# Moving sixteen row tiles of the third image from the last image's attention into the wait for its sorted rows, with a buffer of their own for those rows

## The chip, the core and the metric

The kernel runs on one core of a Trainium2 chip. The metric is the device time of one execution in microseconds. TensorE (PE), VectorE (DVE), ScalarE (ACT), GpSimd (POOL) and SyncE (SP) each run their own list of instructions in order and meet at semaphores. SyncE issues the plain DMAs, GpSimd the indirect ones.

## The reference

Four images of 32 x 32 positions with 128 channels pass three residual blocks, all in float32:

```
x = x + conv(gn(x))            # deformable 3x3 sampling, 8 groups, projected back
t = t + attn(ln(t))            # slices: softmax over the tokens, 8 heads of 32
t = t + moe(ln(ln(t)))         # 8 experts 128 -> 512 -> 128, the best 2 of each token

logits = xt @ Wr + br; top_p, top_idx = top_k(softmax(logits), 2)
xe = xn * ln_g[e] + ln_b[e]
h  = gelu(xe @ W1[e] + b1[e]);  y = h @ W2[e] + b2[e]
out = sum over the two experts of weight * y
```

## The kernel before

The images go through the kernel one after another, and the stages of neighbouring images are woven. Each engine runs one list in which the deformable sampling (conv) of image b is cut into 80 slots, and into these slots the attention, router and expert work of image b - 1 and the last parts of image b - 2 are put. After the last image's conv there is no more conv to weave into: there a tail of slots runs in which `tail_works(slot)` gives two pieces of work, image 3 at table slot `slot + 3` and then image 2 at `slot + 80`.

The tables at the top of the file say at which slot a step stands, and each engine's `work(b, slot)` issues what the tables name. For image 3 the order is: layer norm, the transposes of its normalised tokens, attention (slots 5 to 28), a second norm, the router (35 to 40), ranks and row numbers (43), columns and the b2 product (44 to 47), the scatter of the rows (44 to 55), the load of the rows (56), their transposes and scalings (61 to 63), row tiles (64 to 87), picks (89 to 100), adds (101 to 105).

The expert part works on rows sorted by expert. 1024 tokens with two experts each fill at most ROWS = 23 tiles of 128 rows, each tile of one expert. Its steps, all named in the prediction:

- find_rows (L1738) gives each token its two row numbers (L1760) and each tile its expert.
- sort_rows (L692, POOL, L702) scatters the normalised tokens to `sorted_rows` in DRAM, 16 indirect DMAs of 64 KB.
- load_weights(b, i) (L559, SP, L571 and L573) loads the two weight matrices of tile i's expert, 256 KB each, to a ring. Images 0 to 2 have a ring of 4; image 3 has 12, since 8 more lie in the conv's `asb`, which is free by then. Image 3's first 12 are all issued at WEIGHT_SLOT 45, each further one when a tile before it is done.
- load_rows (L577, SP, L582) brings the sorted rows to SBUF in three pieces. It waits for the scatter and for image 2's results having been stored, since rows come in and results go out through one buffer, `rows_in = rows_out` in `region`.
- turn_rows (L1076, PE, L1083) transposes 4 tiles at a time; scale_rows (L1790, DVE, L1795) applies the expert's norm scale and shift.
- tile(b, i) (L1115, PE) is hidden(i), the four products of L1098, and finish(i - 1), the four of L1111. Between them stands gelu(b, i) (ACT, L1325). After them copy_rows (DVE, L1801). For images 0 to 2 the hidden product has one PSUM bank, so hidden(i) waits for the Gelu of tile i - 1. For image 3 it has four.
- store_rows_out (L588, SP, L590) stores the results in three pieces, pick_rows (L706, POOL, L712) gathers them back in token order, 16 indirect DMAs, and add_rows (L1803, DVE, L1811) adds them with their weights. store_image (L555) ends an image.

The tiles of image 2 (LATE) stand in the tail, at slots 2 to 40 of it, that is 5 to 43 in image 3's table: within image 3's attention and router. Attention steps named in the prediction are the token transposes (L956), logits (L1002, L1003), the two Exps (L1316), the slice sums (L1020), the add of the attention (L1654), the router's transposes (L1040), the ranks (L1053, L1056) and the b2 product (L1072). Between image 3's b2 product and its turn_rows TensorE has nothing in its list.

## Time and profile before

| | |
|---|---|
| median of 3 runs | 1411.14 us (1404.44 to 1413.74) |
| the profiled execution | 1399.52 us |
| its span, first to last instruction | 1397.3 us |
| mean granted TensorE clock | 0.876 |
| busy PE, DVE, ACT, POOL | 75%, 58%, 56%, 48% of the span |
| DMA | 111.11 MB, 80 GB/s on average |

All rows are from the profiled execution, in microseconds from the start of its span. The execution's own time is 2.2 us more than its span and lies below the three timed ones. "Granted clock" is a share of TensorE's full clock: 1.00 is 2.4 GHz and 0.50 is 1.2 GHz.

### The profile page before, as it was taken

What the parts mean: (1) busy time and instruction counts of PE and PEld (TensorE: products, weight loads), DVE (VectorE), ACT (ScalarE), POOL (GpSimd) and SP (SyncE); (2) the same over time, 40 slices, a digit from 0 to 9 for tenths busy, and PEclk for the clock granted to TensorE, in tenths of its full rate; (3) what the DMA queues carried; (4) which work ended last, traced back from release to release, by engine and by line L of the source; (5) the groups of instructions that cost most, each with busy time, mean ns of one, the idle gap of its engine ahead of it and who ended that gap; (6) DMA issues with size and microseconds to landing.
All of it is one profiled execution on the core that took longest, in us unless ns stands there. A gap on an engine that the chain in (4) does not pass through costs nothing.

```text
span 1397.3 us, 51058 instructions
## 1 busy us (share of the span) xinstructions
PE 1050.7 (75%) x22444; PEld 840.0 (60%) x22444; DVE 812.6 (58%) x1609; ACT 786.5 (56%) x1435; POOL 675.3 (48%) x640
## 2 busy tenths in 40 slices
PE   4586858877877878998788679988878776983390
PEld 3465646655565657874577558865656565673390
DVE  5767676756658456565668455566775484434221
ACT  2766666665667355766665636665674553552060
POOL 2755555555445664436645744367456650004404
PEclk9697978988999789999987889999996989997595
DMA  6302121211001332641112125531112201446462
GB/s 159 97 22 53 63 52 63 53 65 36 23 15 31 88 90 83 182 115 41 39 35 86 38 71 151 164 90 30 38 35 85 82 17 32 137 126 197 127 211 58
DMA packets 150524, 111.11 MB, mean 80 GB/s; under 512 B 44009, under 2 KB 131874, under 8 KB 149794
## 3 DMA queue, kind: packets, MB, share of 16 engines
q1 hardware_dynamic: 146210, 99.47, 25.7%
q0 software_dynamic: 4096, 8.40, 2.1%
q8 instruction: 178, 2.92, 0.8%
q14 instruction: 40, 0.33, 0.1%
HBM read 84.17 MB, written 23.66 MB: 77 GB/s over the span
## 4 chain that ended last, share of the span: by engine, by line
PE 54%; ACT 16%; DVE 14%; issue 8%; POOL 3%; SPq 2%; DMA 2%; another core or an unknown queue 1%; POOLq 0%; DVEq 0%; ACTq 0%
PE ps L866 14%; PE ps L850 10%; PE ps L1098 6%; PE ps L874 5%; ACT xsb L1240 5%; PE ps L1111 5%; DVE asb L1572 4%; ACT asb L1258 2%; DVE region L1795 2%; DVE xsb L1549 2%; PE ps L1020 2%; PE ps L823 2%; DMA ring<-in_L_ffn_W 1%; DVE ysb L1563 1%; ACT xsb L1234 1%
## 5 line engine op out<-in xcount | busy, mean ns | idle before, releaser
L741 POOL TENSOR_TENSOR ysb<-ysb,rw 128x576 f32<-128x576 f32 x300 | 336.5, 1143 | 362.4 <-DVE ysb L1563 362.3
L850 PE MATMUL ps<-xsb,ysb 64*64 64x96 f32 x11008 | 340.4, 270 | 100.3 <-issue 25.1
L850 PEld LDWEIGHTS ps<-xsb,ysb 64*64 64x64 f32 x11008 | 283.6, 149 | 170.2 <-issue 97.4
L1240 ACT ACTIVATE xsb<-xsb,pick 128x576 f32<-128x576 f32 (+1 forms) x480 | 336.2, 750 | 5.2
L1572 DVE COPY asb<-ps 128x960 f32<-128x960 f32 (+1 forms) x208 | 215.7, 1043 | 131.0 <-PE ps L866 120.0
L730 POOL TENSOR_TENSOR ysb<-rw,count 128x576 f32<-128x576 f32 (+1 forms) x150 | 176.0, 1173 | 99.2 <-PE ps L850 98.6
L866 PE MATMUL ps<-asb,vd 32*32 32x258 f32 x8192 | 203.0, 393 | 17.3 <-issue 13.8
L1249 ACT ACTIVATE osp<-ps 128x258 f32<-128x258 f32 x128 | 43.0, 444 | 268.7 <-PE ps L866 268.7
L1325 ACT ACTIVATE region<-ps,b_col 128x128 f32<-128x128 f32 x368 | 105.0, 370 | 137.4 <-PE ps L1098 137.3
L866 PEld LDWEIGHTS ps<-asb,vd 32*32 32x32 f32 x8192 | 126.4, 104 | 82.5 <-issue 51.0
L1549 DVE TENSOR_TENSOR xsb<-rw,ps 128x576 f32<-128x576 f32 (+1 forms) x150 | 108.3, 722 | 75.2 <-PE ps L850 57.7
L702 POOL DMA_INDIRECT sorted_rows<-region,row_no x64 | 63.1, 985 | 133.0 <-DVE row_no L1760 116.4
L1234 ACT ACTIVATE xsb<-xsb 128x576 f32<-128x576 f32 (+1 forms) x160 | 105.3, 658 | 21.2 <-DVE xsb L1549 21.2
L1563 DVE SCALAR_TENSOR_TENSOR ysb<-ysb,ps 128x576 f32<-128x576 f32 (+1 forms) x158 | 113.6, 719 | 3.0 <-POOL ysb L730 3.0
L1098 PE MATMUL ps<-region,ring 128*128 128x128 f32 x616 | 93.9, 300 | 27.3 <-ACT region L1325 15.4
L1258 ACT ACTIVATE asb<-ps 128x768 f32<-128x768 f32 x112 | 93.8, 837 | 33.9 <-PE ps L850 28.7
L1098 PEld LDWEIGHTS ps<-region,ring 128*128 128x128 f32 x616 | 81.5, 206 | 39.8 <-issue 29.3
L712 POOL DMA_INDIRECT picked<-expert_rows,row_no x64 | 61.1, 954 | 72.7 <-DMA expert_rows<-region 55.4
L874 PE MATMUL ps<-outw,osp 128*128 128x128 f32 x512 | 78.6, 317 | 12.8 <-issue 7.8
L1581 DVE TENSOR_TENSOR x_tok<-x_tok,ps 128x1024 f32<-128x1024 f32 x32 | 39.0, 1218 | 83.2 <-PE ps L874 80.0
L1111 PE MATMUL ps<-ring,region 128*128 128x128 f32 x616 | 84.2, 281 | 4.0 <-ACT region L1325 4.0
L874 PEld LDWEIGHTS ps<-outw,osp 128*128 128x128 f32 x512 | 72.4, 226 | 18.5 <-issue 14.7
(260 smaller groups left out, 1169.5 us busy)
## 6 DMA issues: line engine op xcount, KB each, us to landing
ring<-in_L_ffn_W SPq DMA_DIRECT2D x154, 256.0 KB
vd<-group_values SPq DMA_DIRECT2D x128, 128.0 KB, 2.7
asb<-in_L_ffn_W SPq DMA_DIRECT2D x30, 256.0 KB
set_rows<-ring SPq DMA_DIRECT2D x4, 1376.0 KB, 6.6
rw<-set_rows SPq DMA_DIRECT2D x30, 172.0 KB, 3.5
group_values<-region SPq DMA_DIRECT2D x32, 128.0 KB, 3.5
region<-sorted_rows SPq DMA_DIRECT2D x8, 512.0 KB
expert_rows<-region SPq DMA_DIRECT2D x8, 512.0 KB
```

Of the source, the lines that this page charges most:

```text
L730: pl.tensor_tensor(ysb[:, ch % DEPTH, 0:sets, NU - 1, :], rows_of(ig)[:, 1, first:first + sets].rearrange("p (s o) -> p s o", o=1) .broadc ...
L741: pl.tensor_tensor(ysb[:, ch % DEPTH, 0:sets, u, :], ysb[:, ch % DEPTH, 0:sets, NU - 1, :], rows_of(ig)[:, 2 + u, first:first + sets].rear ...
L850: last = pe.matmul(ps[64 * j:64 * j + 64, bank + i, NV * GRID * q:NV * GRID * (q + 1)], ysb[rows, ch % DEPTH, col, :, :].rearrange("p u y ...
L866: last = pe.matmul(ps[32 * jc:32 * jc + 32, j, 0:NI * AM], vd[rows, ig % 2, x, :], asb[rows, x, :, :].rearrange("p i n -> p (i n)"), start ...
L874: last = pe.matmul(pcol(project_bank(ig), t), osp[:, ig % 2, t // 4, t // 2 % 2, t % 2 * P:(t % 2 + 1) * P], outw[:, ig % G, :], start=Tru ...
L1098: last = pe.matmul(ps[:, hidden_bank(b, i), j * P:(j + 1) * P], ring_part(r, 0)[:, j * P:(j + 1) * P], xsT[:, i, :], start=True, stop=True)
L1111: last = pe.matmul(ps[:, expert_bank(b, i), 0:C], hT[:, i % 2, j, :], ring_part(r, 1)[:, j * P:(j + 1) * P], start=(j == 0), stop=(j == HJ ...
L1240: act.activation(xsb[:, ch % DEPTH, 0:sets, v, :], xsb[:, ch % DEPTH, 0:sets, NV - 1, :], ACT.Relu, bias=pick[:, v:v + 1], scale=-1.0).the ...
L1258: act.activation(asb[:, :, :, first:first + m].rearrange("p x i m -> p i x m"), ps[:, bank:bank + 2, 0:GRID * m].rearrange("p i (m x) -> p ...
L1549: dve.tensor_tensor(xsb[:, ch % DEPTH, 0:sets, NV - 1, :], rows_of(ig)[:, 0, first:first + sets].rearrange("p (s o) -> p s o", o=1) .broad ...
L1563: dve.scalar_tensor_tensor(v, v, 0.0, units.rearrange("p (o q) -> p o q", o=1) .broadcast_to([P, sets, GRID]), ALU.max, ALU.min).then_inc( ...
L1572: dve.tensor_copy(asb[:, :, :, first:first + m].rearrange("p x i m -> p i x m"), ps[:, bank:bank + 2, 0:GRID * m].rearrange("p i (m x) -> ...
```

## The change

The tables: image 2's first eight tiles stay within image 3's attention and router, at other places (image 3's slots 5, 7, 17, 29, 30, 39, 40, 41), and the other sixteen entries stand at 45 to 60, after the b2 product and before turn_rows. Picks keep their slot number; the adds move by five slots and the store of image 2 by one. Image 3's first twelve weight loads are cut in three lots of four, at slots 52, 57 and 62. The ring numbering of image 3 is turned by four, so that its first eight tiles use the part in `asb`, which image 2 doesn't use, and don't wait for image 2's tiles. Image 3's rows get a place in the conv's `xsb` buffer, both on the way in and on the way out; load_rows then doesn't wait for image 2's stores. turn_rows of image 3 waits for image 2's last copy, as both use PSUM banks 6 and 7.

```diff
-LATE_TILE_SLOTS = tuple(SLOTS + 2 + 5 * i // 3 for i in range(ROWS + 1))
-LATE_PICK_SLOT, LATE_ADD_SLOT, LATE_LAST_SLOT = SLOTS + 53, SLOTS + 72, SLOTS + 82
+LATE_TILE_SLOTS = tuple(SLOTS - TAIL_FIRST + at for at in (5, 7, 17, 29, 30, 39, 40, 41) + tuple(range(45, 61)))
+LATE_PICK_SLOT, LATE_ADD_SLOT, LATE_LAST_SLOT = SLOTS + 53, SLOTS + 77, SLOTS + 83
+LAST_WEIGHT_SLOTS = {52: (0, 4), 57: (4, 8), 62: (8, 12)}
...
-        rows_in = region[:, REGION - ROWS * C:REGION].rearrange("p (i c) -> p i c", i=ROWS)
-        rows_out = rows_in
+        woven_rows = region[:, REGION - ROWS * C:REGION].rearrange("p (i c) -> p i c", i=ROWS)
+        last_rows = x_flat[:, 0:ROWS * C].rearrange("p (i c) -> p i c", i=ROWS)
+
+        def rows_of_tiles(b):
+            return woven_rows if b < B - 1 else last_rows
...
-            r = i % size
+            r = i % size if b < B - 1 else (i + RING) % size
...
             def load_weights(b, i):
...
-                elif b:
+                elif b and r < RING:
                     sp.wait_ge(s.expert_summed, ROWS * b)
...
             def load_rows(b):
                 sp.wait_ge(s.rows_sorted, 16 * TOP * NT * (b + 1))
-                if b:
+                if 0 < b < B - 1:
                     sp.wait_ge(s.expert_stored, 16 * 3 * b)
...
-                if slot == WEIGHT_SLOT:
+                if slot == WEIGHT_SLOT and b < B - 1:
                     for i in range(ahead):
                         load_weights(b, i)
+                elif slot in LAST_WEIGHT_SLOTS and b == B - 1:
+                    for i in range(*LAST_WEIGHT_SLOTS[slot]):
+                        load_weights(b, i)
...
             def turn_rows(b, q):
...
+                if b == B - 1:
+                    pe.wait_ge(s.expert_copied, ROWS * b)
```

`rows_of_tiles(b)` takes the place of rows_in and rows_out in load_rows, store_rows_out, turn_rows and copy_rows.

## Rows read from the trace of the kernel before

**Rows 1.** Stretches of the tail; us, engines busy (instructions), granted clock, DMA share, GB/s

```profile
1168.10:1272.00 103.90, 83.64 (x574) 71.34 (x574) 42.41 (x166) 54.57 (x125) 0.00 (x0) 0.93 0.38 107
1272.00:1310.90 38.90, 2.09 (x17) 1.90 (x17) 6.25 (x16) 0.81 (x1) 29.44 (x31) 0.56 0.82 242
1310.90:1321.00 10.10, 6.08 (x25) 4.59 (x26) 6.31 (x20) 0.00 (x0) 1.35 (x2) 0.50 0.37 94
1321.00:1364.40 43.40, 43.06 (x368) 42.71 (x367) 11.87 (x43) 26.23 (x92) 0.00 (x0) 0.96 0.57 170
1364.40:1397.30 32.90, 0.03 (x1) 0.00 (x0) 4.58 (x17) 0.00 (x0) 15.10 (x16) 0.57 0.22 62
```

**Rows 2.** Waits, 1168 to 1311 us: us in total, times, longest

```profile
PE ps L1083 <- DMA region<-sorted_rows: 35.9, 1, 35.9
...
PE ps L1098 <- ACT region L1325: 15.4, 10, 5.9
```

**Rows 3.** Timeline of GpSimd: start us, us; first and last of 16 scatters

```profile
1272.31 1.00 POOL L702 DMA_INDIRECT sorted_rows<-region,row_no  x1 [116.39 <-DVE row_no L1760]
...
1291.58 0.96 POOL L702 DMA_INDIRECT sorted_rows<-region,row_no  x1 [0.30 <-issue]
```

**Rows 4.** Timeline of SyncE's issues in the wait

```profile
1277.88 0.28 SPq L571 DMA_DIRECT2D ring<-in_L_ffn_W  x1
...
1279.42 0.35 SPq L571 DMA_DIRECT2D ring<-in_L_ffn_W  x1
...
1296.95 0.70 SPq L571 DMA_DIRECT2D asb<-in_L_ffn_W  x1
...
1303.25 0.70 SPq L571 DMA_DIRECT2D asb<-in_L_ffn_W  x1
...
1308.15 2.80 SPq L582 DMA_DIRECT2D region<-sorted_rows  x3
```

**Rows 5.** Groups of ScalarE's instructions, first stretch: busy us, mean ns, idle before

```profile
L1325 ACT ACTIVATE region<-ps,b_col 128x128 f32<-128x128 f32 x92 | 26.2, 368 | 29.6 <-PE ps L1098 29.5
L1325 ACT ACT_TABLE_LOAD x6 | 7.7, 1283 | 0.1
```

**Rows 6.** Timeline, marks of the attention chain

```profile
1182.62 1.04 PE L956 MATMUL ps<-ident,region 128*128 128x128 f32 x8
...
1202.58 1.02 PE L1002 MATMUL ps<-region,ws_bd 128*128 128x512 f32 x2
...
1216.59 1.15 ACT L1316 ACTIVATE xsb<-xsb,a_nmax 128x1024 f32<-128x1024 f32 x1
...
1229.89 4.92 PE L1020 MATMUL ps<-xsb 128*128 128x128 f32 x32
...
1241.64 1.22 DVE L1654 TENSOR_TENSOR x_tok<-x_tok,ps 128x1024 f32<-128x1024 f32 x1 [4.71 <-PE ps L1033]
...
1252.20 1.04 PE L1040 MATMUL ps<-ident,region 128*128 128x128 f32 x8
```

**Rows 7.** Timeline of VectorE, second reciprocal

```profile
1198.16 1.74 DVE L1618 RECIPROCAL ysb<-ysb 128x256 f32<-128x256 f32 x1
```

**Rows 8.** Stretches of 4 us between Exp and slice sums; columns as in rows 1

```profile
1222.00:1226.00 4.00, 1.54 (x13) 1.11 (x11) 1.27 (x7) 3.96 (x8) 0.00 (x0) 0.94 0.46 118
1226.00:1230.00 4.00, 3.65 (x17) 3.69 (x18) 0.00 (x0) 2.25 (x6) 0.00 (x0) 0.50 0.04 13
```

**Rows 9.** Timeline of TensorE, last woven tiles, ranks, b2 product

```profile
1263.52 1.13 PE L1098 MATMUL ps<-region,ring 128*128 128x128 f32 x8 [1.95 <-ACT region L1325]
...
1265.96 1.13 PE L1098 MATMUL ps<-region,ring 128*128 128x128 f32 x8 [0.43 <-ACT region L1325]
...
1267.83 0.34 PE L1053 MATMUL ps<-marks,earlier 128*128 128x72 f32 x2
...
1272.87 2.05 PE L1072 MATMUL ps<-b,region 8*128 8x128 f32 x16 [1.10 <-ACT region L1311]
```

**Rows 10.** Timeline of TensorE, first hidden products of the last image

```profile
1320.78 3.62 PE L1098 MATMUL ps<-region,ring 128*128 128x128 f32 x16
```

More of the change, by code:

```diff
@@ L578, in load_rows @@
                 sp.wait_ge(s.rows_sorted, 16 * TOP * NT * (b + 1))
-                if b:
+                if 0 < b < B - 1:
                     sp.wait_ge(s.expert_stored, 16 * 3 * b)
                 for q in range(3):
-                    sp.dma_start(rows_in[:, CHUNKS[q]:CHUNKS[q + 1], :],
+                    sp.dma_start(rows_of_tiles(b)[:, CHUNKS[q]:CHUNKS[q + 1], :],
                                  sorted_dram.rearrange("(i p) c -> p i c", p=P)[:, CHUNKS[q]:CHUNKS[q + 1], :])\
@@ L590, in store_rows_out @@
                 sp.dma_start(expert_dram.rearrange("(i p) c -> p i c", p=P)[:, CHUNKS[q]:CHUNKS[q + 1], :],
-                             rows_out[:, CHUNKS[q]:CHUNKS[q + 1], :]).then_inc(s.expert_stored, 16)
+                             rows_of_tiles(b)[:, CHUNKS[q]:CHUNKS[q + 1], :]).then_inc(s.expert_stored, 16)
             def work(b, slot):
                 ahead = RING if b < B - 1 else TAIL_RING
-                if slot == WEIGHT_SLOT:
+                if slot == WEIGHT_SLOT and b < B - 1:
                     for i in range(ahead):
+                        load_weights(b, i)
+                elif slot in LAST_WEIGHT_SLOTS and b == B - 1:
+                    for i in range(*LAST_WEIGHT_SLOTS[slot]):
                         load_weights(b, i)
@@ L1082, in turn_rows @@
                 for i in range(4 * q, min(4 * q + 4, ROWS)):
-                    last = pe.transpose(ps[:, 6 + q % 2, i % 4 * P:(i % 4 + 1) * P], rows_in[:, i, :], ident[:, :])
+                    last = pe.transpose(ps[:, 6 + q % 2, i % 4 * P:(i % 4 + 1) * P], rows_of_tiles(b)[:, i, :], ident[:, :])
                 last.then_inc(s.tiles_turned, 1)
@@ L1800, in copy_rows @@
                 dve.wait_ge(s.expert_summed, ROWS * b + i + 1)
-                dve.tensor_copy(rows_out[:, i, :], ps[:, expert_bank(b, i), 0:C]).then_inc(s.expert_copied, 1)
+                dve.tensor_copy(rows_of_tiles(b)[:, i, :], ps[:, expert_bank(b, i), 0:C]).then_inc(s.expert_copied, 1)
             def add_rows(b, m):
```

## The prediction

> **What bounds the kernel now.** I read the stretches first, then the waits, then the timeline around the last two images. In the tail there are five stretches [rows 1]. From 1168.1 to 1272 us the last image's attention and router run, woven with the third image's 23 row tiles; TensorE is busy 83.64 of 103.90 us. From 1272 to 1310.9 TensorE has 2.09 us of work in 38.90. Then come 10.1 us of turning the sorted rows, 43.4 us of the last image's tiles (TensorE busy 43.06) and 32.9 us of picks, adds and store. So the second stretch is a hole, and the first and the fourth are filled by TensorE. The waits name the hole: the first transposes of sorted rows wait 35.9 us for the DMA that loads them [rows 2]. Two things fill this time. GpSimd scatters 16 tiles' rows, from 1272.31, the last issued at 1291.58 [rows 3]. And SyncE has 24 weight loads ahead of the row load, which it reaches only at 1308.15, some 16 us after the last scatter [rows 4]. The rows could not go to their place earlier anyway without the third image's tiles being stored, since both use one buffer.
>
> A second reading of the first stretch matters more. A woven tile is not free there: ScalarE spends 26.2 us on 92 Gelu pieces and reloads its table for them six times at 1283 ns [rows 5], and TensorE's Gelu waits sum to 15.4 us [rows 2]. The attention is a chain, and every tile that stands in it beyond what the chain's own gaps can hold lengthens it.
>
> **The change part by part.** The sum goes by the profiled execution (1399.52 us, span 1397.3). Its time lies below all three timed runs (median 1411.14); I take the gain from its span and subtract it from the median.
>
> *Part A, 16 tiles leave the attention.* I lay the chain out again with the marks of [rows 6], one segment after another. Start to the transpose of the normalised tokens (1182.62): tile 2 goes, worth 2.1 us, as TensorE is slow here. To the first logits (1202.58, 19.96 us): five tiles stand there, one will. Four tiles at some 1.8 us (43.4 us for 23, [rows 1]) would be 7.1, but then the reciprocals' chain on VectorE (1.74 us each half, [rows 7]) ends last: 5.3. To the first Exp (1216.59, 14.0 us): two tiles between the logits and one Gelu go, the Exp table load follows the logits: 4.1. To the slice sums (1229.89, 13.3 us): here Exp and Gelu alternate. Two Gelus of 4 x 368 ns, the table loads between them and a tile go, and some 1 us comes as the transposes run slow (1.04 us at full clock, as at 1182.62): 5.2. (The parts that go add up to more than that; the chain Exp, transpose, copy, Exp, transpose, copy is what stays.) To the attention's add (1241.64, 11.75 us): a tile goes (1.8), sums run slower for longer: -0.3. To the transpose for the router (1252.20, 10.56 us): four tiles become two, 1.7. To the ranks (1267.83, [rows 9], 15.6 us): five tiles become three, but the transposes and router run at the slow clock: -1.2. From the ranks to the row numbers nothing changes. The sum is 16.9, and I take 17.
>
> The clock is the large unknown here. TensorE's granted clock was 0.94 in 1222 to 1226 with 1.54 of 4 us busy, and 0.50 in the next 4 us [rows 8]: a sparse stretch costs the following one half its speed (the 1.2 GHz level instead of 2.4). Before, 11 us at roughly half busy did it. After, between logits and sums TensorE has some 2 of 9 us of work, and again a gap of 4 us before the router's transpose. I have charged 6 us: half the sums (2.2), the transposes (2), the router (1.8; sixteen pieces, as in the b2 product's 2.05). If the clock stayed high the whole way, part A would be worth 22 to 23; if it stayed low from the logits to the ranks, every TensorE piece there doubles: sums and output product 3.8 each (32 pieces, four hidden products' worth of 0.95, [rows 9]), transposes 3, router 1.9, ranks 2 and 5 tiles at 1.1, in all 20 instead of 6, and part A is worth 3.
>
> *Part B, 16 tiles stand in the wait.* A lone tile in this form has a pitch of 2.44 us: hidden product at 1263.52, the next at 1265.96, since one PSUM bank makes it wait for its Gelu [rows 9]. The row numbers are ready at about 1272.0; the b2 product ends at 1274.92 and will end 2.3 us after the row numbers, as one tile's product no longer precedes it. Fifteen hidden products from there: the last starts 2.3 + 14 x 2.44 = 36.5 us after the row numbers. Its Gelu, second product and copy take 3.5: 40. The hole was 38.9 long, so on TensorE alone the hole is filled with nothing over, and the scatter (20.3 us) is no longer what ends last.
>
> *Part C, queues in that wait.* SyncE now holds, in order: late loads 11 to 17, four tiles of the last image (52), late loads 18 to 21, the three row loads (56), late load 22, four more tiles (57), the last store of the third image, and four more (62). One tile's two loads take about 1.6 us to issue (1277.88 to 1279.42, [rows 4]). Load 17 is released some 19 us after the row numbers; the four tiles behind it take 6.4, so load 18 is issued at 28 and lands at 31, while its product is due at 26.7: a stall of 4. Load 22 stands behind 1.5 MB of rows, another 2. The DMA itself can carry this: with 0.82 of it busy it moved 242 GB/s in the hole [rows 1], some 295 when full, and the tiles ask 0.52 MB per 2.44 us, 215 GB/s, plus 52 for the scatter (64 KB per 1.26 us). Part B becomes 46 us. Bounds: 40 with no stall, 52 if each late load waits a queue's length.
>
> *Part D, the buffer, the added wait and the turning.* The rows have their own buffer, so they land long before they are wanted. The transposes now wait for the copy of tile 22 instead; behind them on TensorE is everything of the last image. The turning took 9.9 us, until the first hidden products at 1320.78, at clock 0.50 [rows 1, 10]; 6.31 of it were VectorE's scalings, with a pause while the next rows and transposes came. With all rows there VectorE's scalings set it (some 0.32 us each, 6.31 for 20 pieces); TensorE's last transposes wait for sixteen of them, 5.2, and with the first and the last transposes it is 6.5. Hidden(0) thus starts 46 + 6.5 = 52.5 us after the row numbers, before 48.8. The fourth stretch starts warm: 1.9 less (3.62 us for the first two products, [rows 10], instead of twice 0.95).
>
> The clock gate rule of the Trainium skill (TensorE: Matmul & The Clock Gate, Part 4: PE-mode transpose) says that transposes do not count as activity for the clock. The trace agrees so far: all of the turning ran at 0.50 [rows 1]. By that rule the 1.9 of the warm start would be lost and the gain would be 13.
>
> *The rest.* The third image's picks (20 us on GpSimd) move into the last tiles; GpSimd has nothing else there, and they end about 67 us after the row numbers, before the adds at tile 16 (81). Their adds, 16 on VectorE, stand beside tiles that leave it idle most of the time (11.87 busy of 43.4, [rows 1]). The picks, adds and store at the end stay at 32.9. Moving them costs nothing unless the picks come 14 us late. The turned ring numbering only lets the last image's first eight tiles use the upper buffers.
>
> *Sum.* 17 (A) - 3.7 (B, C and the turning) + 1.9 (warm start) = 15.2, 15 us. Span 1382, that execution 1384.5; from the median 1411.1 - 15 = 1396.
>
> ScalarE's table price is another place where page and trace differ. Of ScalarE's 29.6 us of idle time ahead of Gelu pieces 29.5 are waits for TensorE [rows 5], so a load costs its 1283 ns and nothing more. The Trainium skill (ScalarE: Activation LUTs, What ACT_TABLE_LOAD costs) adds a drain of about 1380 ns to each switch; by it the five loads that go would bring up to 7 us more, an estimate from that page. I go by the trace.
>
> **The rivals.**
> *The clock eats it.* The attention without its tiles stays at the low level from logits to ranks. For it: [rows 8], and that it took only half-idle stretches before. Against: the sums and products are themselves 8 us of dense work, and the clock came back within 4 to 8 us of such work. Part A is worth 3 and the sum 1: 1410.
>
> *The SyncE queue becomes the bound, on the slow side.* From about 1295 to 1308 each SyncE instruction took some 0.70 us; the load at 1296.95 was followed by the next at 1303.25, a pitch of 6.3 us per tile, with the DMA far from full [rows 4]. It set in after some 12 closely spaced loads under GpSimd's indirect DMAs. Before, nobody waited for these loads but the row load. Now the third image's tiles do. If it sets in with the burst of slot 52, loads 18 to 22 have 6.3 instead of 2.44 (19 us), the row load adds 4 and its neighbour 4: 27 - 15, 12 slower: 1423. It decides against the change from the point where four loads are at that pace. Against it: loads are now released one per tile, and elsewhere with GpSimd busy SyncE was quick.
>
> *More than forecast.* The clock stays high, and the four-tile burst doesn't stall load 18: 22.5 + 2.3 - 1.9, and 4 more for the stall: 24 to 27 us, 1386.
>
> *It trades place for place.* If the hole had only been long because SyncE was slow (the rows could have been there at about 1298), a run in which it is quick gains 12 less: 1408.
>
> **How the numbers follow.** Forecast 0.52 (its own range 1389 to 1403), clock 0.14, trade 0.12, SyncE 0.08, more 0.14. Two in ten are cut off about equally on both sides: 1384 to 1411. A measurement here tells about 1% (14 us) from nothing. The forecast lies on that edge, so half of it counts as faster, with all of "more" and a little of "trade" (runs differ): 0.26 + 0.14 + 0.03, and I say 0.45. Slower is SyncE and the worst of the clock: 0.10. Same: 0.45.
>
> **What would show it.** Right: the row numbers come about 17 us earlier; the clock row shows a dip in the attention before the sums and before the router; Gelu's table loads fall from six to three; in the wait TensorE has some 2 us of 2.44 busy, with one pause near tile 18 and one near tile 22; the transposes of sorted rows wait for VectorE's copy or nothing, not for the DMA; the last 32.9 us unchanged. Wrong: row numbers less than 8 us earlier (clock), waits of TensorE for ring loads over 10 us in the wait (SyncE), or a hole that stays.

## The result, and the profile after

The changed kernel took 1436.99 us (median of 4 runs, 1429.37 to 1454.15), the kernel before beside it 1407.79 (1399.08 to 1413.74). The ratio, without slow executions such as the one of 1454.15 (in e4 and e5 it is the profiled one that was slow, but its extra time lies ahead of the tail), is 1.0163, 95% interval 1.0105 to 1.0222: slower, by one to two percent. 1396 was forecast, with 1384 to 1411 as the range. The profiled execution took 1434.3 us, its span is 1432.1; 1384.5 was forecast for it.

The five stretches of the tail, in the same cut as [rows 1]: the attention and router, the wait with its 16 tiles, the turning, the last image's tiles, and picks, adds and store. Columns: length, busy time of TensorE, its weight loads, VectorE, ScalarE and GpSimd with the number of instructions, granted clock, share of the DMA engines, GB/s.

```profile
1174.70:1262.40 87.70, 62.36 (x327) 49.28 (x328) 38.66 (x151) 32.18 (x60) 0.00 (x0) 0.79 0.15 43
1262.40:1333.10 70.70, 43.39 (x265) 40.74 (x265) 10.38 (x29) 17.10 (x60) 15.45 (x16) 0.78 0.69 200
1333.10:1339.80 6.70, 4.02 (x23) 3.03 (x24) 5.99 (x19) 0.00 (x0) 2.70 (x3) 0.83 0.90 242
1339.80:1399.10 59.30, 47.90 (x370) 47.13 (x368) 12.12 (x43) 26.12 (x92) 12.44 (x14) 0.85 0.55 159
1399.10:1432.10 33.00, 0.04 (x1) 0.00 (x0) 4.58 (x17) 0.00 (x0) 15.11 (x16) 0.55 0.22 62
```

Against before the attention is 16.5 us shorter (104.2 from its last convolution product to the row numbers, now 87.7), as forecast. The wait and the turning went from 48.4 to 77.4, where 52.5 was forecast. The last image's tiles went from 43.7 to 59.3, where 41.8 was forecast (43.7 less the 1.9 of the warm start). The end is the same. With 6.6 us more in the body ahead of the tail, which no edit touches and which differs by up to 31 us between the traces of this study (the tail starts between 1161.5 and 1192.2), these make the 34.8 us between the two spans. So the result stands in two places: the tiles in the wait, and the last image's tiles, from which nothing had been moved.

What the engines wait for there, as sums from 1174.7 us on (total, times, longest):

```profile
ACT region L1335 <- remote: 26.6, 3, 11.6
DVE xsb L1811 <- remote: 17.8, 2, 12.3
DVE region L1811 <- remote: 13.7, 1, 13.7
PE ps L1108 <- DMA ring<-in_L_ffn_W: 11.1, 2, 6.3
PE ps L1121 <- ACT region L1335: 9.4, 2, 9.1
```

"Remote" is a release that the profile can pin on no instruction of the core. ScalarE's Gelu (L1335) and VectorE's copy (L1811) wait so for 58 us in six waits; each counts from the engine's last instruction, so the first microseconds of it may be ordinary waiting for a product. The timeline of the wait shows where they stand (start us, us, engine, line):

```profile
1270.23 1.06 PE L1121 MATMUL ps<-ring,region 128*128 128x128 f32 x8
1270.93 0.71 SPq L576 DMA_DIRECT2D ring<-in_L_ffn_W  x1
1271.38 0.96 POOL L710 DMA_INDIRECT sorted_rows<-region,row_no  x1 [0.30 <-issue]
...
1275.97 1.14 ACT L1335 ACTIVATE region<-ps,b_col 128x128 f32<-128x128 f32 x4 [6.89 <-remote]
...
1277.25 2.05 PE L1108 MATMUL ps<-region,ring 128*128 128x128 f32 x8 [5.96 <-ACT region L1335]
...
1281.48 0.96 POOL L710 DMA_INDIRECT sorted_rows<-region,row_no  x1 [0.30 <-issue]
1285.17 0.29 DVE L1811 COPY region<-ps 128x128 f32<-128x128 f32 x1 [13.73 <-remote]
1285.19 1.14 ACT L1335 ACTIVATE region<-ps,b_col 128x128 f32<-128x128 f32 x4 [8.09 <-remote]
...
1285.61 2.05 PE L1121 MATMUL ps<-ring,region 128*128 128x128 f32 x8 [6.31 <-DVE region L1811]
```

The 16 scatters run from 1262.42 to 1282.44 without a gap but GpSimd's own 0.30 us. The tile before passes beside them at its usual pace. The product of the next tile ended at about 1270.4, yet its Gelu starts at 1275.97. A second product whose copy was due at about 1271.3 is copied at 1285.17, and at 1285.19 the next Gelu starts: both engines are let go together, 2.7 us after the last scatter. In these 14 us TensorE gets one hidden product done, and that one and the next at half clock (2.05 us for 8 pieces instead of 1.06).

The same again under the third image's 16 picks, which also run unbroken, 1336.49 to 1356.20:

```profile
1353.59 0.29 DVE L1811 COPY xsb<-ps 128x128 f32<-128x128 f32 x1 [12.27 <-remote]
...
1355.26 0.94 POOL L720 DMA_INDIRECT picked<-expert_rows,row_no  x1 [0.30 <-issue]
1359.28 2.17 ACT L1335 ACTIVATE region<-ps,b_col 128x128 f32<-128x128 f32 x8 [11.63 <-remote]
...
1360.47 2.07 PE L1121 MATMUL ps<-asb,region 128*128 128x128 f32 x8 [9.09 <-ACT region L1335]
```

Between the two stand TensorE's waits for weights, from the same timeline:

```profile
1305.26 0.37 SPq L578 DMA_DIRECT2D asb<-in_L_ffn_W  x1
1306.73 0.36 SPq L576 DMA_DIRECT2D ring<-in_L_ffn_W  x1
...
1311.25 2.08 PE L1108 MATMUL ps<-region,ring 128*128 128x128 f32 x8 [6.29 <-DMA ring<-in_L_ffn_W]
...
1316.66 3.66 SPq L587 DMA_DIRECT2D xsb<-sorted_rows  x3
1321.08 1.00 SPq L576 DMA_DIRECT2D ring<-in_L_ffn_W  x1
...
1327.36 2.08 PE L1108 MATMUL ps<-region,ring 128*128 128x128 f32 x8 [4.81 <-DMA ring<-in_L_ffn_W]
```

Each is a late load of the third image that SyncE issues only behind loads of the last image (the one at 1306.73 behind four tiles' loads, the one at 1321.08 behind the three row loads). These are the two pauses of part C, 4 and 2 us there.

In the kernel before the 16 scatters and the 16 picks of the third image made one train of 32, from 1272.3 to 1312.5, while TensorE, ScalarE and VectorE had next to nothing to do until 1310.9 [rows 1, 3]. What it held up was SyncE, whose slow instructions I had seen [rows 4] and read as a matter of SyncE, and at its end VectorE's last scalings (under part D).

### The profile page after: what moved, and what is told of

Same layout as the page of the kernel before. It is cut to its first block, busy times and chain, and to the rows that moved or that the text cites. A ratio compares the mean times of both kernels' runs of the same rounds, so it can differ in the third digit from the quotient of the medians.

```text
span 1432.1 us, 51055 instructions
## 1 busy us (share of the span) xinstructions
PE 1078.2 (75%) x22444; PEld 862.2 (60%) x22444; DVE 814.1 (57%) x1609; ACT 780.2 (54%) x1430; POOL 672.4 (47%) x640
## 4 chain that ended last, share of the span: by engine, by line
PE 55%; DVE 16%; ACT 15%; issue 7%; another core or an unknown queue 3%; DMA 2%; SPq 1%; POOL 1%; POOLq 0%; DVEq 0%; ACTq 0%
PE ps L874 14%; PE ps L858 11%; PE ps L1108 6%; PE ps L882 5%; PE ps L1121 5%; ACT xsb L1250 4%; DVE asb L1582 4%; DVE xsb L1559 2%; DVE ysb L1573 2%; ACT asb L1268 2%; DVE region L1805 2%; PE ps L831 2%; PE ps L1028 1%; DMA ring<-in_L_ffn_W 1%
## 5 line engine op out<-in xcount | busy, mean ns | idle before, releaser
L858 PE MATMUL ps<-xsb,ysb 64*64 64x96 f32 x11008 | 346.4, 274 | 98.4 <-issue 25.9
L858 PEld LDWEIGHTS ps<-xsb,ysb 64*64 64x64 f32 x11008 | 289.2, 152 | 168.6 <-issue 99.7
L1582 DVE COPY asb<-ps 128x960 f32<-128x960 f32 (+1 forms) x208 | 215.9, 1044 | 138.6 <-PE ps L874 126.7
L1335 ACT ACTIVATE region<-ps,b_col 128x128 f32<-128x128 f32 x368 | 104.8, 370 | 152.5 <-PE ps L1108 108.7
L1108 PE MATMUL ps<-region,ring 128*128 128x128 f32 x608 | 97.5, 310 | 39.8 <-ACT region L1335 16.9
L1108 PEld LDWEIGHTS ps<-region,ring 128*128 128x128 f32 x608 | 83.8, 213 | 49.8 <-issue 26.8
L1121 PE MATMUL ps<-ring,region 128*128 128x128 f32 x608 | 89.0, 294 | 11.9 <-DVE region L1811 7.6
L1121 PEld LDWEIGHTS ps<-ring,region 128*128 128x128 f32 x608 | 82.4, 210 | 13.1 <-issue 8.2
```

What stands on the lines that cost most here:

```text
L858: last = pe.matmul(ps[64 * j:64 * j + 64, bank + i, NV * GRID * q:NV * GRID * (q + 1)], ysb[rows, ch % DEPTH, col, :, :].rearrange("p u y ...
L1108: last = pe.matmul(ps[:, hidden_bank(b, i), j * P:(j + 1) * P], ring_part(r, 0)[:, j * P:(j + 1) * P], xsT[:, i, :], start=True, stop=True)
L1121: last = pe.matmul(ps[:, expert_bank(b, i), 0:C], hT[:, i % 2, j, :], ring_part(r, 1)[:, j * P:(j + 1) * P], start=(j == 0), stop=(j == HJ ...
L1582: dve.tensor_copy(asb[:, :, :, first:first + m].rearrange("p x i m -> p i x m"), ps[:, bank:bank + 2, 0:GRID * m].rearrange("p i (m x) -> ...
```

## The experiments

Three theories. TRAIN: a long unbroken run of GpSimd's indirect DMAs holds up what the other engines wait for until it is over. LOADS: late weight loads behind SyncE's others set the pace. CLOCK: the low granted clock does. The table has each kernel's tail by the same marks, read from one timeline of each, in us: from the start of the last convolution product to the first scatter, when the row numbers are there (A), on to the first transpose of sorted rows (B), on to the first hidden product (turning), on to the end of the last product (C), and the rest. The ratios are to the kernel before, run beside: its medians were 1411.64 us beside e1 to e4, 1415.78 beside e5 to e8 and 1399.92 beside e9 to e12, so times of different groups are not to be compared.

```
kernel                          A     B    turn    C    end   tail
before                        104.2  38.5   9.9  43.7  32.9  229.2
changed                        87.7  70.7   6.7  59.3  33.0  257.4
e1  scatters in fours          87.7  62.2   6.7  60.2  32.9  249.6
e2  and picks in fours         87.9  63.1   6.7  48.3  32.9  238.8
e3  late loads first           87.6  58.2   6.4  64.2  32.9  249.4
e4  all three                  87.5  48.7   6.7  54.5  32.9  230.3
e5  picks spread wider         87.5  46.9   6.7  50.7  33.7  225.6
e8  four scatters only         87.5  58.8   6.8  60.2  32.8  246.0
e9  plain transfers            89.2  62.1   6.7  60.2  32.9  251.1
e10 tiles left in place       101.0  26.0  20.5  44.2  32.9  224.6
e11 scatters with rests        87.3  61.9   6.6  58.7  32.8  247.3
e12 before, rows sooner       101.0  25.7  20.9  44.1  32.9  224.5
e6  ten tiles in the wait      96.6  39.8   7.3  47.2  33.7  224.6
e7  before, rows sooner,      101.0  25.9   7.3  48.1  33.6  215.9
    picks spread
```

**Scatters in fours (e1).** Groups two to four wait until 9, 12 and 15 tiles of the third image are summed.

```diff
+                if b == B - 1 and m in (4, 8, 12):
+                    pl.wait_ge(s.expert_summed, ROWS * LATE + (9, 12, 15)[m // 4 - 1])
                 pl.indirect_dma_start(sorted_dram,
```

> The changed kernel, with the last image's 16 scatters in four lots of four; lots two to four each wait until one more of the third image's tiles is done (tiles 8, 11, 14). Same DMAs, same bytes. Theory TRAIN (a long unbroken run of indirect DMAs on GpSimd holds up semaphore waits and instructions of VectorE, ScalarE and SyncE until it ends): the two idle stretches of TensorE of about 6 us each near tiles 9 and 10 go, the hidden product of the last image's tile 0 starts 12 to 18 us sooner after the row numbers than the 77.6 us of the changed kernel; about 1420 us. The episode in the picks stays. Theory LOADS (the stalls come from the order and amount of weight loads): the stretch stays at 70 us or more. Theory CLOCK (the clock alone makes the tiles slow): no change.

Measured: 1430.43 us, ratio to before 1.014 (1.0085 to 1.0194). The interval overlaps that of the changed kernel, so the whole time alone doesn't show a gain; the tail does, with 7.8 us instead of the 12 to 18 expected. B fell from 70.7 to 62.2, and of the three stalls under the scatters only a pause of 3.5 us behind the last group is left, though GpSimd now needed 31.7 us for what it did in 20.0. The waits for weights (the first of them longer than the 6.3 us before) and the stall under the picks stayed:

```profile
1300.72 1.14 ACT L1337 ACTIVATE region<-ps,b_col 128x128 f32<-128x128 f32 x4 [3.47 <-remote]
...
1307.83 2.07 PE L1110 MATMUL ps<-region,ring 128*128 128x128 f32 x8 [8.35 <-DMA ring<-in_L_ffn_W]
...
1323.50 2.08 PE L1110 MATMUL ps<-region,ring 128*128 128x128 f32 x8 [4.77 <-DMA ring<-in_L_ffn_W]
```

**Picks in fours too (e2).** The same wait ahead of the third image's picks 4, 8 and 12, until 2, 6 and 9 tiles of the last image are summed.

```diff
+                if b == LATE and m in (4, 8, 12):
+                    pl.wait_ge(s.expert_summed, ROWS * (B - 1) + (2, 6, 9)[m // 4 - 1])
                 pl.indirect_dma_start(picked[:, m, :], None, expert_dram,
```

> As the scatter in fours, and the third image's 16 picks also in lots of four, which wait for tiles 1, 5 and 8 of the last image. TRAIN: the stall of 9 us at the last image's second and third tile goes too, the last image's tiles take 44 us or less in place of 59.3, so another 12 to 16 us; about 1405 us. LOADS: the last image's tiles stay at 55 us or more, since their loads stand where they stood. CLOCK: no change.

Measured: 1415.76 us, ratio 1.0034 (0.9999 to 1.007). C fell from 60.2 to 48.3, in the stretch that the edit touches and in no other; 44 or less was expected.

**Late loads first (e3).** The last image's loads go to slots 58, 59 and 62, the row load to 57, so that no late load of the third image stands behind four tiles of the last.

```diff
-LAST_WEIGHT_SLOTS = {52: (0, 4), 57: (4, 8), 62: (8, 12)}
+LAST_WEIGHT_SLOTS = {58: (0, 4), 59: (4, 8), 62: (8, 12)}
+LAST_ROW_SLOT = 57
```

> The changed kernel with another order of loads on SyncE and no other change: all loads of the third image's tiles, then the row load, then the last image's first four tiles (slots 57, 58, 59 in place of 56, 52, 57). LOADS: both waits of TensorE for ring loads (6.3 and 4.8 us) and the cold tiles behind them go and most of the rest with them, 20 us or more; about 1415 us. TRAIN: the two waits for the ring go, 11 us plus up to 5 of slow products, but the two 6 us stalls near tiles 9 and 10 and the 9 us one in the last tiles stay; about 1422 us.

Measured: 1424.19 us, ratio 1.0106 (1.007 to 1.0142). B is 58.2. The waits for weights are gone but for 2.8 us in two (2.16 the longer), and those for the train stand as they were, to within some tenths:

```profile
1281.79 1.14 ACT L1336 ACTIVATE region<-ps,b_col 128x128 f32<-128x128 f32 x4 [6.88 <-remote]
...
1290.35 0.29 DVE L1812 COPY region<-ps 128x128 f32<-128x128 f32 x1 [13.13 <-remote]
```

C rose by 4.9. Its trace shows where: the third image's 16 picks, which began 3.3 us before the last image's first hidden product in the changed kernel (1336.49, 1339.82), begin 8.2 us behind it here (1341.03, 1332.88). So all of the train and the release behind it now lie on the last tiles, and TensorE's longest wait for a Gelu there is 13.87 us instead of 9.09:

```profile
1363.80 2.17 ACT L1336 ACTIVATE region<-ps,b_col 128x128 f32<-128x128 f32 x8 [15.21 <-remote]
...
1364.99 2.07 PE L1122 MATMUL ps<-asb,region 128*128 128x128 f32 x8 [13.87 <-ACT region L1336]
```

**All three (e4).**

> Scatter and picks in fours and the other order of loads together. TRAIN with the load order as a second, separate cost: all three add up, 12 to 18 plus 12 to 16 plus 11 to 16 us, so 1390 to 1400 us, below the kernel before (about 1408). If one cause lies behind all stalls, e4 is no better than the better of e2 and e3 by more than 5 us.

Measured: 1404.65 us, ratio 0.9953 (0.9917 to 0.9989), slower than the 1390 to 1400 expected. B is 48.7: of the 22.0 us below the changed kernel's 70.7, the scatters in fours alone gave 8.5 and the loads alone 12.5, so the two are nearly independent. C is 54.5, not 48.3: the picks' first condition had long been met, so that two groups ran together as eight:

```profile
1343.59 0.97 POOL L725 DMA_INDIRECT picked<-expert_rows,row_no  x1 [31.14 <-DMA expert_rows<-region]
1344.86 0.96 POOL L725 DMA_INDIRECT picked<-expert_rows,row_no  x1 [0.30 <-issue]
...
1352.37 0.94 POOL L725 DMA_INDIRECT picked<-expert_rows,row_no  x1 [0.30 <-issue]
1355.46 0.95 POOL L725 DMA_INDIRECT picked<-expert_rows,row_no  x1 [2.16 <-remote]
```

TensorE then waited 6.66 us for a Gelu; behind the later groups of four it was about 1.

**Picks spread wider (e5).** All three, with the groups at 9, 13 and 17 finished tiles of the last image, the third image's adds and store behind them (slots 81 and 86), and a DRAM buffer of its own for the last image's results, so that its stores need not wait for the picks.

```diff
-                if b:
+                if 0 < b < B - 1:
                     sp.wait_ge(s.rows_picked, 16 * TOP * NT * b)
-                sp.dma_start(expert_dram.rearrange("(i p) c -> p i c", p=P)[:, CHUNKS[q]:CHUNKS[q + 1], :],
+                sp.dma_start(results(b).rearrange("(i p) c -> p i c", p=P)[:, CHUNKS[q]:CHUNKS[q + 1], :],
...
+                    pl.wait_ge(s.expert_summed, ROWS * (B - 1) + (9, 13, 17)[m // 4 - 1])
```

> All three remedies, with the picks' lots now released by tiles 8, 12 and 16 of the last image, so that a real gap of 2 us or more stands between lots (in the run before the first two lots ran together as eight), the third image's adds moved behind tile 20, and a DRAM buffer of its own for the last image's results, so that SyncE doesn't wait for the picks. TRAIN: the stall of 6.7 us in the last tiles goes; they take 44 to 47 us in place of 54.5, the tail from the last projection to the end 221 to 224 us (before: 229.2). If the stall comes from anything else at that place (loads, clock) it stays above 52.

Measured: 1408.88 us, ratio 0.9955 (0.9912 to 0.9999), which is no other time than that of e4. In its trace C is 50.7, not the 44 to 47 expected, and each group of four is followed by a stall of 1 us (0.98, 0.94 and 1.03; 2.54 at the first).

**Fewer scatters (e8).** The last image's scatters 4 to 15 are left out, and the row load waits only for the four; most of its rows are thus those of the image before.

```diff
+                if b == B - 1 and m >= 4:
+                    return
                 pl.indirect_dma_start(sorted_dram,
```

> The changed kernel with only the first 4 of the last image's 16 scatters; 12 are left out, so its rows are mostly the third image's. No pause is added and nothing else changes. TRAIN: no stall of 6 us near tiles 9 and 10, the stretch from row numbers to the first transposes of sorted rows falls from 70.7 to 58 to 64 us, as with the scatter in fours (62.2). If the waits that pace the fours had done it rather than the broken train, it stays at 70. The 9 us stall in the picks stays either way.

Measured: one run, 1437.45 us, where the kernel before took 1415.78 on the same chip. One run says little of the whole time, which is no better than the changed kernel's. B is 58.8, and no engine waits on anything remote in it. So it isn't the pauses of e1 that help, but that no long train runs. The waits for weights (6.66 and 5.02 us) and the stall under the picks (12.13) stayed, as expected.

**Scatters with rests (e11).** A memset of 128x1280 behind each scatter, which waits for nothing but the one before.

```diff
+                if b == B - 1:
+                    if m:
+                        pl.wait_ge(s.paused, m)
+                    pl.memset(y_flat[:, 1536:2816], 0.0).then_inc(s.paused, 1)
```

> The changed kernel with a GpSimd memset of 128x1280 (about 1.2 us) behind each of the last image's scatters, so that these come every 2.5 us or so and none waits for a tile: 40 us for the 16 in place of 20. TRAIN, in the form that it is the closeness of the scatters (no gap between them): no stall over 2 us at the tiles beside them, and the stretch to the turning is 60 to 66 us, as with scatters in fours. In the form that GpSimd's indirect transfers merely have to be many in flight or in number: stalls of 6 us or more come again, and since the scatters last twice as long the stretch is 75 us or more. CLOCK: 70.7 as in the changed kernel.

Measured: one run, 1419.18 us, before 1399.92. B is 61.9. GpSimd is busy without a pause for 35.7 us, with the same 16 scatters, but they come at a pitch of 2.3 us instead of 1.26:

```profile
1262.15 0.96 POOL L710 DMA_INDIRECT sorted_rows<-region,row_no  x1 [0.16 <-issue]
1263.10 1.19 POOL L716 MEMSET ysb<- 128x1280 f32 x1
1264.46 0.97 POOL L710 DMA_INDIRECT sorted_rows<-region,row_no  x1 [0.17 <-issue]
...
1279.75 0.29 DVE L1815 COPY region<-ps 128x128 f32<-128x128 f32 x1 [2.16 <-PE ps L1125]
1282.20 0.29 DVE L1815 COPY region<-ps 128x128 f32<-128x128 f32 x1 [2.16 <-PE ps L1125]
1284.65 0.29 DVE L1815 COPY region<-ps 128x128 f32<-128x128 f32 x1 [2.16 <-PE ps L1125]
```

VectorE's copies come every 2.45 us under them, the undisturbed pace of a tile. So it is the closeness of the scatters that matters, and not their number alone. Nor were the DMA engines merely full: their share was 0.38 while the changed kernel was held up (1270.0 to 1285.2) and 0.94 here, from 1270 to 1293, without a hold-up. The waits for weights are still there, 7.65 and 7.36 us long.

**Plain transfers (e9).** 16 plain GpSimd DMAs of the same tiles in place of the scatters; the rows then stand in the wrong places of the row store.

```diff
+                if b == B - 1:
+                    pl.dma_start(sorted_dram[m * P:(m + 1) * P, :], xn_tok[:, t, :]).then_inc(s.rows_sorted, 16)
+                    return
```

> The changed kernel with the last image's 16 indirect scatters put as 16 plain GpSimd DMAs of the same 128x64 tiles to 16 whole tiles of the row store (the rows therefore stand in the wrong places, and the outcome is not the reference's). TRAIN, in the form that indirect addressing does it (16 scatters each of which keeps GpSimd busy with 128 row addresses): the first stalls, 6.9 us at the Gelu of tile 9 and about 8 us at the copy of tile 10, are gone, and the stretch from the row numbers to the turning shrinks from 70.7 to about 60 (what it was with four scatters, 58.8, and with scatters in fours, 62.2). TRAIN, in the form that any dense row of GpSimd DMAs does it: the stalls stay, 6 us or more each, and the stretch stays at 68 to 71. LOADS and CLOCK, by which the stalls come from the weight loads or from the granted clock: the stretch stays at about 70.7 in either form. The ring waits (6 and 5 us) and the stall under the picks (12 us) stay in all.

Measured: one run, 1414.61 us, before 1399.92. B is 62.1, and no wait on anything remote stands in it.

```profile
1250.68 8.61 POOL L711 DMA_DIRECT2D sorted_rows<-region  x16 [101.75 <-DVE row_no L1773]
```

They are even closer, 16 in 8.61 us. But that makes the train shorter too: it ends where the indirect one had only begun to disturb. So the run speaks for the indirect form and does not prove it.

**Tiles left in place (e10).** The changed kernel with the old places of the third image's tiles and adds; the buffer and the new order of loads stay.

```diff
-LATE_TILE_SLOTS = tuple(SLOTS - TAIL_FIRST + at for at in (5, 7, 17, 29, 30, 39, 40, 41) + tuple(range(45, 61)))
-LATE_PICK_SLOT, LATE_ADD_SLOT, LATE_LAST_SLOT = SLOTS + 53, SLOTS + 77, SLOTS + 83
+LATE_TILE_SLOTS = tuple(SLOTS + 2 + 5 * i // 3 for i in range(ROWS + 1))
+LATE_PICK_SLOT, LATE_ADD_SLOT, LATE_LAST_SLOT = SLOTS + 53, SLOTS + 72, SLOTS + 82
```

> The changed kernel with the third image's 24 tiles and its additions back at the slots they had before; the row buffer of its own and the reordered weight loads of the last image stay. TRAIN: the move is what costs and gains; without it the part up to the row numbers is back at 101 to 104 us, no tile stands under the scatters, the picks again run beside the wait, and the stretch to the turning is 30 to 39, since the last loads are no longer held by tiles; the time is 1390 to 1408, no slower than before. If instead the buffer or the reordered loads cost something by themselves (the unpredicted term lies there): the last part from hidden(0) to the last finish is over 46 us against 43.7 before, or the stretch to the turning over 40, and the time is over 1412.

Measured: 1396.47 us, ratio 0.9992 (0.9963 to 1.0022): the whole loss hangs on the move. B fell from 38.5 to 26.0 (30 to 39 was expected), as the rows are now loaded ahead of most of the weights, but the turning took 20.5 instead of 9.9.

**The kernel before with its rows loaded sooner (e12).** Only four of the twelve weight loads stay ahead of the row load.

```diff
-                if slot == WEIGHT_SLOT:
-                    for i in range(ahead):
+                if slot == WEIGHT_SLOT or (b == B - 1 and slot == ROW_SLOT + 1):
+                    for i in range(ahead) if b < B - 1 else range(0, 4) if slot == WEIGHT_SLOT else range(4, ahead):
```

> The kernel before with one edit: of the last image's first twelve weight loads only four are issued ahead of the load of the sorted rows, the other eight behind it. SyncE's slow issues under the train (0.70 us per instruction) then stand behind the row load: the wait from the row numbers to the first row transpose falls from 38.5 to about 26 (what it was in the combination with spread picks), and the time to 1395 to 1401. If the picks of the third image, which still come as an unbroken train of 32 with the scatters, hold back the row load as well, the stretch stays over 32 and the time within 0.4% of before. What is left to the combination's 1393.9 is then the worth of the spread picks.

Measured: 1397.08 us, ratio 0.9967 (0.9933 to 1.0002). The rows came as early as expected, B 25.7, and most of it was lost at once: the turning, which the expectation had forgotten, now stands under the picks' part of the train.

```profile
1297.04 1.97 PE L1083 MATMUL ps<-ident,region 128*128 128x128 f32 x8 [23.06 <-DMA region<-sorted_rows]
...
1305.96 1.36 DVE L1795 TENSOR_SCALAR region<-ps,scale_col,shift_col 128x128 f32<-128x128 f32 x4 [5.05 <-remote]
...
1310.77 0.95 POOL L712 DMA_INDIRECT picked<-expert_rows,row_no  x1 [0.30 <-issue]
...
1315.77 3.59 DVE L1795 TENSOR_SCALAR region<-ps,scale_col,shift_col 128x128 f32<-128x128 f32 x11 [8.44 <-remote]
```

VectorE's scalings and TensorE's transposes wait here, two instructions that no tile and no weight load has to do with. One scaling is released at 1305.96 in the midst of the train, the last ones 4.1 us behind the last pick.

**Ten tiles in the wait (e6), and the winner (e7).** e6 is e5 with 13 of the third image's tile places in the attention instead of eight (eleven entries stay in the wait, ten hidden products and the last finish), the scatters' groups at 14, 17 and 20 finished tiles, and the first loads at slot 54. e7 is e12 with e5's picks, adds, store and buffer for the last image's results: no tile moved.

```diff
-LATE_TILE_SLOTS = tuple(SLOTS - TAIL_FIRST + at for at in (5, 7, 17, 29, 30, 39, 40, 41) + tuple(range(45, 61)))
+LATE_TILE_SLOTS = tuple(SLOTS - TAIL_FIRST + at for at in (5, 7, 10, 13, 17, 26, 28, 29, 30, 39, 40, 41, 42) + tuple(range(45, 56)))
```

> As e5, but only 10 tiles of the third image stand in the wait and 13 in the attention. A tile in the attention costs the path about 1.0 us (16.4 us saved by 16), a tile in the wait 2.44 once the wait is longer than the scatter needs. TRAIN with this price: attention 92 to 95 us (87.6 with eight tiles, 104.2 with 23), row numbers to the first transposes 32 to 36 (48.7), last tiles 44 to 47, whole tail 207 to 215 us and some 1390 us. If the saving of the attention is not linear in the tiles, the attention is at 98 or more and the tail no better than e5.

> The kernel before, with tiles where they were, but only 4 of the 12 tiles' weight loads ahead of the row load on SyncE, the third image's picks in spread fours beside the last tiles and a DRAM buffer of its own for the last results. The hole was long since SyncE was slow under a train of 32 indirect DMAs and had 24 loads to issue. With this the first transposes start 25 to 30 us after the row numbers in place of 38.5, the rest as before: tail 217 to 222 us, about 1400 us. If the hole is set by the scatter's landing or the DMA's fill, it stays at 35 or more.

Measured: e6 1402.06 us, ratio 0.9936 (0.9884 to 0.9988), with a tail of 224.6 where 207 to 215 was expected: A (96.6) and B (39.8) are each longer than forecast. e7 1393.89 (1391.64 to 1399.67), ratio 0.9849 (0.9792 to 0.9907), faster than both kernels. Its wait, turning and tiles:

```profile
1276.70:1302.60 25.90, 2.05 (x16) 1.86 (x16) 6.01 (x15) 0.54 (x1) 19.53 (x20) 0.57 0.55 174
1302.60:1310.00 7.40, 5.94 (x24) 4.46 (x25) 6.15 (x19) 0.00 (x0) 0.00 (x0) 0.50 1.12 313
1310.00:1358.00 48.00, 44.43 (x369) 43.47 (x368) 10.22 (x36) 26.08 (x92) 11.35 (x12) 0.96 0.72 218
```

With the train cut after four picks the turning takes 7.3 us instead of e12's 20.9; the other 12 picks cost 4 us among the tiles (48.1 against 44.1). The tail is 13.3 us shorter than before, and 4.7 with the early rows alone (e12). But 3.2 of each is the attention (A, 104.2 against 101.0), which neither edit touches. From the row numbers on it is 10.1 for both together (125.0 against 114.9) and 1.4 for the early rows alone. The ratio of e7 stands for some 21 us; what lies beyond the tail is not explained.

## Why the prediction was wrong

*Part A, forecast 17: right in mechanism, the number in part by luck.* The row numbers came 16.5 us earlier. The clock did what was charged: both Exp transposes at 1.97, the sums at 5.99 (7.7 at half clock throughout), the router at 3.58, while the output product kept the full clock (3.84). The Gelu table loads fell from six to three. The later runs set the size right, though: three traces with the tiles in their old places (e7, e10, e12) have 101.0 us, since in the profiled execution of before the tile ahead of the sums and the sums had run into a low clock that those did not meet (4.92 us for the sums against 3.74 in e12). Against these the move is worth 13.3.

*Part B, "a lone tile in this form has a pitch of 2.44 us": the step that failed.* The pitch is right where nothing disturbs (2.45 under e11's scatters). But I took it from a stretch in which GpSimd did nothing, and put the tiles beside a train of scatters, under which the kernel before had no tile at all. The cost had to be bounded from the nearest row, which was SyncE's slowness in the same train, and I read that as SyncE's own. Of SyncE's four instructions between 1295 and 1308, moreover, only the two in [rows 4] took 0.70; the other two are recorded with 0.00. The stalls cost 8.5 us (e1), up to 12 (e8), where the sum had nothing. Even with the train broken and the loads in order the stretch is 46.9 (e5) and not 40: the b2 product ran at half clock (3.68 us instead of 2.05) and ended 3.5 us after the first scatter, and single hidden products still waited 0.5 to 2 us for weights.

*Part C, "a stall of 4" and "another 2": mechanism right, size off.* The two stalls came at the places named, as 6.3 and 4.8 us, with slow products behind each (2.08 and 1.92 us for 8 that take 1.13 and 1.06). Taking their cause away gave 12.5 us (e3), where 6 stood. Both stalls were taken too short (11.1 together), and the clock behind a stall was left out.

*Part D.* The turning took 6.7 us, 6.5 forecast. The warm start (1.9) did not come:

```profile
1339.82 3.62 PE L1108 MATMUL ps<-region,asb 128*128 128x128 f32 x16
```

This is the same 3.62 as in [rows 10], although the last tile's product ran at full clock (1.13 us) until 0.5 us before the turning. The granted clock was 0.83 over the turning and 0.50 in its last 1.8 us, in 1.61 of which TensorE was busy with transposes. By the clock gate rule of the Trainium skill (TensorE: Matmul & The Clock Gate, Part 4: PE-mode transpose) transposes do not count as activity, and by it this gain would be lost; the trace agrees. Other runs spread: the same 16 pieces took 2.84 us in e6 and 2.89 in e2, so up to 0.8 of the 1.9 came there. The 9.9 us of before was not only VectorE's pace and a pause for rows, as I had read it. VectorE stood idle for 2.6 us ahead of its last scalings, although the transposes that they needed had ended at 1315.95, and began them 4.8 us behind the train:

```profile
1317.32 4.96 DVE L1795 TENSOR_SCALAR region<-ps,scale_col,shift_col 128x128 f32<-128x128 f32 x15 [2.60 <-PE ps L1083]
```

*The rest, "moving them costs nothing unless the picks come 14 us late": failed.* I asked when the picks would be done and not what runs under them. Moved out of the idle wait into the last image's tiles, they cost 11.9 us (C of e1 against e2) of the 15.6 that C grew. The remaining 3.7 were not taken apart; each group of four still cost about 1 us (waits of 1.31, 1.30 and 0.90 us in e2).

*Sum.* In the tail 24.9 us went wrong at the wait and turning, 17.5 at the last tiles, 0.5 at the attention and 0.1 at the end; with 6.6 in the body these are 49.6 of the 49.8 that lie between 1384.5 and 1434.3, the rest being the 15.2 that was rounded to 15.

*The rivals.* The sum of "more than forecast" adds 2.3 and takes 1.9 away; by the forecast's own terms it is 22.5 - 3.7 + 1.9 + 4 = 24.7, within its 24 to 27. Nearest to the outcome was the SyncE queue on the slow side. It had the right row, [rows 4], and the right place, but the wrong carrier: SyncE's loads kept their pace (1.6 us a tile at 1300 to 1308) outside the train, and even with them out of the way (e3) the stalls remained. CLOCK fell as the first cause with e11: no edit to TensorE's work, and 8.8 us less. It follows the stalls and adds to them.

The mechanism stays open. No run shows what the release stands behind; "remote" says only that the profile found no releaser. Nor was a plain train of 20 us tried.

## What to carry to other kernels

Work put into an idle stretch shares it with whatever else runs there: list what every queue does in the hole, GpSimd's indirect DMAs first, before counting it as free. Where many gathers or scatters are due, spread them in fours behind tile counts or put work between them. And before tiles are moved into a wait, ask why the wait is long: here two changes of order and one more buffer, with no tile moved, gave a ratio of 0.9849, and the move at its best 0.9936. The two intervals just overlap; the tails, 215.9 and 224.6 us, tell them apart.

## What the runs showed of the hardware

- From about the seventh of 16 unbroken scatters (1.26 us each) on, and from about the sixth of 16 picks, ScalarE and VectorE are held up for 5 to 14 us with work that is ready, and TensorE behind them.
- Some are let go in the midst of the train (1275.97 and 1353.59 in the changed kernel, 1305.96 in e12). The last come 2.7 to 4.8 us behind the end of its last instruction (2.7 in the changed kernel's wait, 3.1 under its picks, 4.1 in e10 and e12, 4.8 in before).
- SyncE's DMA instructions take 0.70 us under such a train instead of 0.35, in before from 1281.46 us on (0.68), the eighth scatter. Single ones are as long without any train (0.81 us at 1310.93 and 1.00 at 1321.08 in the changed kernel), so that sign alone doesn't prove a train.
- Length and closeness both matter: behind four in a row TensorE waits about 1 us (2.5 at the first group in e5), behind eight 6.7, and with 16 at a pitch of 2.3 us not at all, as far as the waits show.
